# Causal attention with scores as 64-row pairs, output rows straight from turned weights, z on GpSimd, and the next part's loads issued in its last sixteen batches

## What is computed

```python
def _mha(q, k, v):                                   # part c: q = layernorm(x), k = v = ctx, 16 heads of 32 channels
    scores = einsum('bhqd,bhkd->bhqk', qh, kh) / sqrt(hd)
    causal = ki <= qi
    scores = where(causal, scores, -10000.0)
    attn = softmax(scores, axis=-1)
    out = einsum('bhqk,bhkd->bhqd', attn, vh)
x = x + _mha(_layernorm(x), ctx_2048, ctx_2048)
x = x + _L1_ffn_ref(_layernorm(x), workspace, ...)   # part d: starts from all of part c's x
```

## Time and profile before

| | us |
|---|---|
| median of 3 runs | 3930.52 |
| the profiled execution | 3928.73 |
| its span, first to last instruction | 3926.6 |
| TensorE busy in the span | 3598.9 (92%) |
| VectorE busy | 2855.4 (73%) |
| ScalarE busy | 2566.4 (65%) |
| GpSimd busy | 1624.4 (41%) |

### The profile page before, as it was taken

How to read it: one execution, slowest core, us unless ns; L and a number is a source line. 1 busy time by engine, 2 the same in 40 slices (tenths; PEclk the granted TensorE clock), 3 DMA queues, 4 the chain that set the end, 5 groups by cost and what they waited for, 6 DMA issues and landing times. The chain is left out here.

```text
span 3926.6 us, 86340 instructions
## 1 busy us (share of the span) xinstructions
PE 3598.9 (92%) x24389; PEld 1800.9 (46%) x24451; DVE 2855.4 (73%) x4503; ACT 2566.4 (65%) x6417; POOL 1624.4 (41%) x2090
## 2 busy tenths in 40 slices
PE   5999999999999999699999889999995899999997
PEld 1222222222222222477777644444443665566664
DVE  5888888888888889577777667777774446464655
ACT  2777777777777777577776667777774454545454
POOL 6444444444444441566666322222222234242524
PEclk9999999999999999899999999999997999999999
DMA  7777777777777774333333223333334022030402
GB/s 117 122 123 122 122 124 124 122 121 124 121 122 124 123 144 112 109 114 109 110 110 105 70 90 95 97 90 93 97 91 147 11 66 66 26 106 3 130 1 76
DMA packets 344192, 390.16 MB, mean 99 GB/s; under 512 B 58640, under 2 KB 223120, under 8 KB 343952
## 3 DMA queue, kind: packets, MB, share of 16 engines
q1 hardware_dynamic: 317328, 352.82, 41.0%
q10 hardware_dynamic: 26624, 34.63, 3.4%
HBM read 200.65 MB, written 84.93 MB: 73 GB/s over the span
## 5 line engine op out<-in xcount | busy, mean ns | idle before, releaser
L372 DVE TENSOR_REDUCE a_neg_max<-a_max_ps 128x2 f32<-128x1024 f32 x1024 | 1200.1, 1219 | 189.2 <-PE a_max_ps L461 165.6
L493 ACT ACTIVATE a_P<-a_ring_ps 128x512 f32<-128x512 f32 x2048 | 1084.4, 602 | 382.4 <-PE a_ring_ps L443 378.1
L461 PE MATMUL a_max_ps<-a_K,a_Q 96*128 96x512 bf16 x2048 | 620.8, 384 | 44.9 <-DMA a_K<-a_k_split 39.5
L443 PE MATMUL a_ring_ps<-a_Q,a_K 98*128 98x512 bf16 x2048 | 617.6, 382 | 5.0 <-DMA a_Q<-a_max_rows 2.9
L478 PE MATMUL a_pv_ps<-a_P,a_V 128*32 128x512 f32 x4096 | 544.9, 604 | 1.8 <-ACT a_out_sb L498 1.8
L443 PEld LDWEIGHTS a_ring_ps<-a_Q,a_K 98*128 98x128 bf16 x2048 | 157.8, 96 | 657.8 <-ACT a_P L493 584.4
L1181 ACT ACTIVATE c_P<-c_s_ps,c_bias 128x128 f32<-128x128 f32 x1024 | 362.2, 367 | 138.3 <-DVE c_bias L1053 128.1
L1110 PE MATMUL c_s_ps<-c_KD,c_qT 128*128 128x512 f32 x512 | 276.7, 622 | 33.4 <-ACT c_qT L1172 28.8
L1049 DVE TENSOR_REDUCE c_neg_max<-c_s_ps 128x4 f32<-128x512 f32 x256 | 175.5, 685 | 163.5 <-PE c_s_ps L1111 163.5
L461 PEld LDWEIGHTS a_max_ps<-a_K,a_Q 96*128 96x128 bf16 x2048 | 182.3, 98 | 224.9 <-DVE a_neg_max L372 47.5
L319 POOL TENSOR_SCALAR a_var_eps<-a_mean_var 128x1 f32<-128x1 f32 x64 | 12.3, 192 | 644.5 <-DVE a_mean_var L388 644.2
(11 more groups left out here) (251 smaller groups left out, 7084.0 us busy)
## 6 DMA issues: line engine op xcount, KB each, us to landing
a_Q<-a_q_split SPq DMA_DIRECT2D x384, 128.0 KB, 4.6
a_K<-a_k_split SPq DMA_DIRECT2D x384, 128.0 KB, 7.4
heads_out<-a_out_sb ACTq DMA_DIRECT2D x128, 256.0 KB, 3.6
a_x_in<-in_x_dram SPq DMA_DIRECT2D x64, 256.0 KB, 3.6
a_c_in<-in_ctx_dram SPq DMA_DIRECT2D x64, 256.0 KB, 4.1
a_cT_in<-in_ctxT_dram SPq DMA_DIRECT2D x64, 256.0 KB, 4.0
b_x_in<-in_x_dram SPq DMA_DIRECT2D x64, 256.0 KB, 2.8
b_o_in<-heads_out SPq DMA_DIRECT2D x64, 256.0 KB
```

What stands on the lines that cost most here:

```text
L372: dve.tensor_reduce(neg_max[:, p, 2 * u:2 * u + 2], max_ps[u % 2][:, :, :], AX.X, ALU.max, negate=True).then_inc(max_taken, 1)
L443: pe.matmul(ring(s, use_of(k))[:, :], K[i][:, h, n:n + 128], Q[i][:, h, :], start=True, stop=True).then_inc(scores_filled, 1)
L461: last = pe.matmul(max_ps[u % 2][:, j, :], Q[i][0:KROW, h, m:m + 128], K[i][0:KROW, h, :], start=True, stop=True)
L493: act.activation(P[p][k // NT][:, k % NT, :], ring(s, use_of(k))[:, :], ACT.Exp, scale=SCALE).then_inc(exp_done, 1)
```

## The change

1. **Scores.** `KD` keeps two heads a row group (half the size). A chunk's scores are two fp32 matmuls of 64 rows and 256 columns, rows 0 to 63 and 64 to 127, into two banks, and the mask is added by two bf16 matmuls of 256 columns. The four banks now hold two chunks, so S(c) waits for the exps of chunk c - 2.
2. **Output.** `products` has PT as the stationary operand (128 columns) and 32 columns of V moving, and writes output rows directly. The turn of oT and its ScalarE copy are gone; the last chunk's products are issued in the next step, behind S(0).
3. **z on GpSimd**, as the last instruction of its step, in stage 0 instead of stage 1.
4. **Order.** TensorE turns z at c = 2 instead of at the end, and multiplies with `after` at c = 0 instead of c = 1; ScalarE copies qT before the exps of c = 2; VectorE weighs the `after` product at c = 1 and takes moments at c = 3.
5. **The seam.** Part d's tensors and the semaphores that this needs move to a `WorkspaceState` that lives over both parts. SP issues the five weights in steps 48 to 52, the small loads in steps 53 to 56, X in steps 57 to 60. GpSimd does the memsets in step 56 and rstd and x_r in step 64. VectorE makes the constants in steps 57 to 59, the moments of X[0] in steps 60 to 63 and normalises it in steps 64 to 67. For this SP's last 16 steps and GpSimd's and VectorE's last 8 before the drain are written out too.

```diff
-def causal_attention(nc, x, ctx, ctxT, ident, after, causal_cols, x_out):
+def causal_attention(nc, x, ctx, ctxT, ident, after, causal_cols, x_out, w):
...
-        KD = [sb(f"KD{i}", [128, CK, G, 128], F32) for i in range(2)]
+        KD = [sb(f"KD{i}", [128, CK, 2, 128], F32) for i in range(2)]
...
-        s_ps = ps("s_ps", [128, CK, G, 128], F32)
+        s_ps = ps("s_ps", [128, 2, 2, 512], F32)
...
                     for h in range(G):
-                        sp.dma_start(KD[i][h * D:(h + 1) * D, :, h, :],
+                        sp.dma_start(KD[i][h * D:(h + 1) * D, :, h % 2, :],
...
-            pipeline(sp, B, 5, step)
+                if 48 <= t.k < 53:
+                    dst, src = w.big[t.k - 48]
+                    sp.dma_start(dst, src).then_inc(w.big_in, 16)
+                if 53 <= t.k < 57:
+                    for dst, src in w.small[(t.k - 53) * 6:(t.k - 52) * 6]:
+                        sp.dma_start(dst, src).then_inc(w.small_in, 16)
+                if 57 <= t.k < 61:
+                    i, h = (t.k - 57) // 2, (t.k - 57) % 2
+                    for b in range(h * 4, h * 4 + 4):
+                        sp.wait_ge(x3_stored[b % 2], (i * 4 + b // 2 + 1) * 16)
+                        sp.dma_start(w.X[i][:, b, :], w.x[i * 8 + b]).then_inc(w.x_loaded[i][h], 16)
+            pipeline(sp, B, 5, step, ahead=16)
...
                     held.wait_ge(rstd_done, b + 1)
-            pipeline(pool, B, 5, step)
+                    at_least(held, qT_filled, b - 1)
+                    pool.tensor_scalar(z[:, i, :], x_in[:, t.slot(0, 8), :], mean_var[:, i, 0:1], rstd[:, i:i + 1], ALU.subtract, ALU.mult).then_inc(z_done, 1)
+                if t.k == 56:
+                    for n, (dst, value) in enumerate(w.presets):
+                        pool.memset(dst, value).then_inc(w.preset, 1)
+                        pool.wait_ge(w.preset, n + 1)
+                if t.k == 64:
...
+            pipeline(pool, B, 5, step, ahead=8)
...
-                    if t.exists(3) and c == 2:
+                    if t.exists(3) and c == 1:
...
-                    if t.exists(1) and c == 0:
-
-                        b, i, j = t.batch(1), t.slot(1, 2), t.slot(1, 8)
-                        dve.wait_ge(rstd_done, b + 1)
-                        at_least(dve, qT_filled, b - 1)
-                        dve.tensor_scalar(z[:, i, :], x_in[:, j, :], mean_var[:, i, 0:1], rstd[:, i:i + 1], ALU.subtract, ALU.mult).then_inc(z_done, 1)
-                    if t.exists(0) and c == 1:
+                    if t.exists(0) and c == 3:
...
+                if 60 <= t.k < 64:
+                    j = t.k - 60
+                    dve.wait_ge(w.x_loaded[0][j // 2], 64)
+                    for b in range(2 * j, 2 * j + 2):
+                        dve.bn_stats(w.stats[:, b, :], w.X[0][:, b, :]).then_inc(w.stats_done, 1)
...
+                if 64 <= t.k < 68:
+                    dve.wait_ge(w.rstd_done, 1)
+                    for b in range(2 * t.k - 128, 2 * t.k - 126):
+                        dve.tensor_scalar(w.X[0][:, b, :], w.X[0][:, b, :], w.moments[:, b, 0:1], w.rstd[:, b:b + 1],
+                                          ALU.subtract, ALU.mult).then_inc(w.z_done, 1)
...
-                        at_least(pe, exp_done, (b - 1) * H + (c + 1) * G)
-                        pe.matmul(s_ps[:, c], qT[i][:, c, :], KD[i][:, c], start=True, stop=False)
-                        pe.matmul(s_ps[:, c], identb[:, :], farb[:, :].unsqueeze(1).to_broadcast([128, G, 128]),
-                                  start=False, stop=True).then_inc(s_filled, 1)
+                        at_least(pe, exp_done, b * H + (c - 1) * G)
+                        for r in range(2):
+                            rows = slice(r * 64, r * 64 + 64)
+                            pe.matmul(s_ps[:, c % 2, r, 0:256], qT[i][rows, c, :], KD[i][rows, c], start=True, stop=False)
+                        for r in range(2):
+                            last = pe.matmul(s_ps[:, c % 2, r, 0:256], identb[:, :], farb[:, :].unsqueeze(1).to_broadcast([128, 2, 128]),
+                                             start=False, stop=True)
+                        last.then_inc(s_filled, 1)
                     if t.exists(4) and c == 0:
-
-                        b, i = t.batch(4), t.slot(4, 2)
-                        pe.wait_ge(oT_done, b + 1)
-                        for k in range(CK):
-                            last = pe.transpose(bank_b[:, k, :], oT[:, i, k, :], identf[:, :])
-                        last.then_inc(o_filled, 1)
+                        products(t, 4, CK - 1)
...
-                    last = pe.matmul(bank_b[g * D:(g + 1) * D, c, :], V[t.slot(3, 4)][:, h * D:(h + 1) * D], PT[i][:, h, :],
+                    last = pe.matmul(bank_b[:, h * D:(h + 1) * D], PT[i][:, h, :], V[t.slot(back, 4)][:, h * D:(h + 1) * D],
...
-                if t.exists(3):
-                    b, i = t.batch(3), t.slot(3, 2)
-                    act.wait_ge(oT_filled, b + 1)
-                    at_least(act, o_filled, b - 1)
-                    act.activation(oT[:, i], bank_b[:, :, :], ACT.Copy).then_inc(oT_done, 1)
```

More of the change, by code:

```diff
@@ new lines, in step @@
+                if 60 <= t.k < 64:
[3 more added lines that the diff above has]
+                        dve.bn_stats(w.stats[:, b, :], w.X[0][:, b, :]).then_inc(w.stats_done, 1)
+                    for b in range(2 * j, 2 * j + 2):
+                        dve.wait_ge(w.stats_done, b + 1)
+                        dve.bn_aggr(w.moments[:, b, :], w.stats[:, b, :]).then_inc(w.moments_done, 1)
@@ L1095, in _ @@
+                if 64 <= t.k < 68:
[3 more added lines that the diff above has]
+                                          ALU.subtract, ALU.mult).then_inc(w.z_done, 1)
+            pipeline(dve, B, 5, step, ahead=8)
         @block.tensor
@@ L1127, in step, with products @@
                         if c > 0:
-                            products(t, c - 1)
-                        if c == 1:
-                            pe.wait_ge(qT_done, min(b + 2, B) if isinstance(b, int) else b + 2)
-                            pe.matmul(bank_a[:, :, :], after_sb[:, :], V[t.slot(3, 4)][:, :], start=True, stop=True).then_inc(mv_filled, 1)
-                if t.exists(1):
-                    b, i = t.batch(1), t.slot(1, 2)
-                    pe.wait_ge(z_done, b + 1)
-                    at_least(pe, masked_v_done, b - 1)
-                    for c in range(CK):
-                        last = pe.transpose(bank_a[:, c, :], z[:, i, c * 128:(c + 1) * 128], identf[:, :])
-                    last.then_inc(qT_filled, 1)
-                if t.exists(3):
-                    products(t, CK - 1)
-            def products(t, c):
-                b, i = t.batch(3), t.slot(3, 2)
+                            products(t, 3, c - 1)
+                    if t.exists(3) and c == 0:
+                        b = t.batch(3)
+                        pe.wait_ge(v_loaded[t.slot(3, 4)], t.lap(3, 4) * 16 + 16)
+                        pe.wait_ge(qT_done, min(b + 2, B) if isinstance(b, int) else b + 2)
+                        pe.matmul(bank_a[:, :, :], after_sb[:, :], V[t.slot(3, 4)][:, :], start=True, stop=True).then_inc(mv_filled, 1)
+                    if t.exists(1) and c == 2:
+                        b, i = t.batch(1), t.slot(1, 2)
+                        pe.wait_ge(z_done, b + 1)
+                        at_least(pe, masked_v_done, b - 1)
+                        for k in range(CK):
+                            last = pe.transpose(bank_a[:, k, :], z[:, i, k * 128:(k + 1) * 128], identf[:, :])
+                        last.then_inc(qT_filled, 1)
+            def products(t, back, c):
+                b, i = t.batch(back), t.slot(back, 2)
                 if c == 0:
-                    pe.wait_ge(v_loaded[t.slot(3, 4)], t.lap(3, 4) * 16 + 16)
                     at_least(pe, o_sum_done, b)
@@ L1422, in step @@
             def step(f, u, after):
-                if f.exists() and not f.second():
+                if f.exists() and not f.second() and f.k != 0:
                     e = f.eight()
@@ L1581, in normalise @@
                                           ALU.subtract, ALU.mult).then_inc(z_done, 1)
-                first = f.exists() and not f.second()
+                first = f.exists() and not f.second() and f.k != 0
                 if first:
@@ L1977, in decoder @@
         ternary_ffn(nc, x, ffn, x2)
[L1978 to L1980 removed]
+    with ExitStack() as st:
+        w = WorkspaceState(nc, st, x3, ident, workspace, compete_wT, compete_b, write_wT, write_b, wq, wkT, wvT, in_proj_cols,
+                           out_wT, out_b, pre_cols, norm_post)
+        causal_attention(nc, x2, ctx, ctxT, ident, after, causal_cols, x3, w)
+        workspace_ffn(nc, x3, w, out)
 def kernel(**inputs):
```

200 lines of the change are left out of this document (111 added, 89 removed).

## The result

The new kernel takes 3835.34 us (median of 4 runs, 3834.83 to 3841.88), the old one beside it 3928.59 (4 runs): ratio 0.9767, with a 95% interval of 0.975 to 0.9784. It is faster, as forecast, and inside the range, but the gain is 93 us where the forecast had 50, and the time lies 5 us under what the prediction called its likeliest case alone (3840 to 3905). The profiled spans stand 94.1 us apart (3926.6 and 3832.5).

What follows compares the result with a forecast made beforehand. TensorE's program order, with two holes per batch, was taken to bound the causal part. 3928.7 - 32 (step) - 28.4 (seam) - 1.8 (memsets) + 11 (last steps) + 0.6 (semaphores) = 3878 us, range 3805 to 3968.

Steps and rivals of the forecast that it cites:

- Seam: Start of part d: TensorE begins about 0.4 us after the barrier, at 3004.3 instead of 3032.75; -28.4 us.
- The last steps: Last sixteen causal batches: VectorE's borrowed constants and moments delay P^T's first copy 1.6 us in seven steps; +11 us.
- The step: One causal batch on TensorE: 10.8 us instead of 11.31, over 63 batches; -32 us.
- P = 0.92: A chunk's products: eight passes at 0.115 us each, 0.92 us instead of 0.36.
- T = 0.53: A chunk's four transposes of P on TensorE: 0.53 us, before and after.
- S = 0.90: A chunk's scores with mask: 0.90 us, with 0.25 for entering and leaving 64-row mode; bounds 0.75 and 1.08.
- KD's smaller memsets: Ahead of the first loads: two memsets of 3.67 us halve as KD is half as large; -1.8 us.
- One more clearing of semaphores: At the kernel's end: one additional clearing; +0.6 us.
- Rival 1: Causal batches: GpSimd's z shuts VectorE out, TensorE stands 1.45 us a batch, step 12.25, 3960 us; chance 0.22.
- Rival 2: Products: full weight loads not hidden, at least 192 ns a pass, step 13.3, 4020 us; chance 0.05.
- Rival 3: Products: weight loads cheap, 0.08 us a pass, step 9.7, 3808 us; chance 0.12.
- Rival 4: Scores: 64-row pairs don't overlap, 1.08 us or more a chunk, step 11.5, 3922 us; chance 0.05.

Runs made afterwards that it cites:

- Run 3: New kernel with z moved back from GpSimd to VectorE, in the next step's first chunk: 3828.85 us (0.9747).
- run 4: New kernel with each chunk's scores again one product of 128 rows and 512 columns, two banks in turn: 3869.31 us (0.9853).
- run 2: Old kernel's causal batches, with the next part's loads, memsets, constants and moments in their last sixteen steps as in the change: 3912.18 us (0.9955).
- run 11: New kernel with the next part's VectorE, GpSimd and SP work spread over the last sixteen steps: 3828.26 us (0.9742).
- run 10: New kernel with qT turned at the end of the step again (TensorE and ScalarE at c = 3): 3891.92 us (0.99).
- run 5: New kernel with products as before (V as weight), the result turned back, ScalarE's copy of oT ahead of exp(0): 3788.49 us (0.9646).
- run 6: New kernel plus one unread VectorE bn_stats per batch ahead of total, so total starts under GpSimd's z: 3874.23 us (0.9859).
- run 7: run 6 with GpSimd's z replaced by two tensor_tensor additions, results not the reference's: 3914.95 us (0.9966).
- run 8: run 5 with ScalarE's copy of qT behind the exps of chunk 2 instead of ahead: 3786.65 us (0.9636).

## Why the prediction was right, and where its size was wrong

- **The bound.** PE's program order set the step before and sets it after. Shown by runs 3 and 4: a full us more on DVE changes nothing, 0.64 more on PE changes the step by 0.64.
- **Seam.** -28.4 forecast, -28.6 found. Run 2 shows it for itself, less its late steps.
- **The last steps.** +11 forecast, +8 found. That DVE's lump delays P^T's first copy was right, and run 11 shows it. The forecast's 1.6 us a step, seven times, was not: it lets POOL's z hold `bias` and `total` on top. In the trace z held `bias` behind the first two lumps (0.68 at 2838.80 and 2849.73) and neither of the two behind the last four (0.23 each). Six steps lost 0.4 to 1.4 us, and one lost 3.2, with a wait of 1.17 us and the slow clock behind it, which the forecast did not have. That the sum came near is partly luck.
- **The step, -32 forecast, some -70 found.** This is the sum whose terms were mis-sized. The largest error is **P = 0.92**. The rate was nearly right: 0.115 a pass forecast, 0.112 found. But the forecast charged it eight times, and it is paid seven times, because the first load of a group runs under the transposes in front: 0.031 + 7 x 0.112 = 0.81. That is -0.11 x 4 = -0.44. The second is **T = 0.53**. That figure of the earlier trace rows was read with products in column groups behind it, and holds the way into them. The same timeline of before has a T with full scores behind it, and there, up to the scores at 2402.82, it takes 0.43:

```profile
2402.39 0.60 PE L1125 MATMUL c_pT_ps<-c_identf,c_P 128*128 128x128 f32 x4
```

In the new kernel T is 0.44, so -0.09 x 4 = -0.36, and -0.06 on the turn of z. Against these stands **S = 0.90**, which is 0.97 with its way in: +0.07 x 4 = +0.28. So T and S nearly cancel: the price of the way in stood in T where it belonged to S. 10.79 - 0.44 - 0.36 - 0.06 + 0.28 = 10.21, and 10.19 is measured. The low bound of the step, 9.95, held it.
- **Parts of the 70.** Undone one at a time, the pairs are worth 34 us (run 4), the place of z's turn 57 (run 10) and the products -47 (run 5): 44 together. The other 26, with the vanished wait for oT's copy among them, no run has for itself, and such parts need not add up.
- **Holes.** That qT's copy is hidden by the new place was argued with 0.3 us to spare; the trace has no wait, and run 10 brings it back at 1.0 us a step. The move stands for more than the "0.52" that the rows of before showed.
- **KD's smaller memsets.** They take 1.96 instead of 3.67, but the stretch from the part's first memset to S(0) is 11.37 us, 0.29 longer than before. The first z on POOL lasts 2.07 where DVE took 0.55, and while the pipeline fills nothing covers it. Run 3, with z back on DVE, has 9.41 there, 1.7 less than before. So the -1.8 was right and z on POOL took it away; the fill was left out of the sum.
- **One more clearing of semaphores, +0.6.** No run shows this term. Behind the seam the new trace is 0.35 us shorter, and the time around the span is 2.3 instead of 2.1.
- **Rival 1** (z shuts DVE out) was not met in the steady stretch, because `total` starts 0.44 ahead of z (2603.55 and 2603.99). Had it been met, its price was wrong: by run 6 it is 0.55 at most, within P^T's slack of 0.64, and not 1.45. The earlier trace rows showed the lock with an addition, and run 7 shows it with additions again; I had carried it to an instruction of another form. The Trainium skill (SBUF — State Buffer, "SBUF: two separate sides") speaks of an exclusive lock between DVE and GpSimd. Run 7 agrees with it (2609.75 beside 2609.73), run 6 only for z's first 0.78 us.
- **Rival 2** (full loads not hidden, 0.192 a pass) is refuted by 0.112. (Its 4020 was also added wrongly: 3878 + 32 + 126 is 4036.) The rule of the Trainium skill (TensorE: Matmul & The Clock Gate, Part 3, "The mechanism") that a load overlaps matmuls only in another row group does not hold here: these loads and passes are all in one. The same section also has loads pulled ahead into a background weight buffer, which would fit.
- **Rival 3**'s 3808 is nearer to 3835 than the forecast's 3878, but its cause is not what happened: a pass takes 0.112, not 0.08. **Rival 4** (pairs don't overlap) is refuted by run 4 and by the starts 0.007 us apart.

## What to carry to other kernels

Read an operation's length between the neighbours that it will have: the same transposes took 0.53 ahead of column groups and 0.44 ahead of full ones. Where a run of equal passes is paced by its weight loads, count the intervals and not the passes, as the first load can lie under what runs in front: eight passes took 0.81 and not 8 x 0.115. Undo each part of a bundle for itself: this one won by the order of its instructions, the scores and the seam, while the part that seemed its centre, output rows without turning, cost 47 us against turning them with the copy in a better place. Work borrowed from the next stage belongs in the idle places of a step, one piece each, and not at its end in a lump.

## What the runs showed of the hardware that was not expected

- A GpSimd addition of 128x512 holds a DVE `scalar_tensor_tensor` of 128x16 until it ends (run 7); a GpSimd `tensor_scalar` with two scalars per row (mean and rstd), 2.08 us long, holds it only until 0.78 us behind its own start (run 6).
- The DVE's own z of 128x512 takes 0.54 us in the first three batches of the kernel before, with GpSimd idle, and 0.96 to 1.00 in most others, where it starts some 0.35 us into GpSimd's multiplication.
- A 128-column fp32 weight load shows as 192 ns but allows a new pass every 0.112 us, if 32 columns move.
- Ahead of 64-row groups the last pass in front takes 0.09 to 0.10 us longer (the product with `after`, the turns and the products all show it). A pass of 256 columns in a pair takes 0.31 where a full one takes 0.215. Full fp32 scores behind 32-column passes also start 0.09 slower.
- One PE wait of 1.17 us was followed by some 7 us at a granted clock of 0.50, and one of 1.06 (run 6, at 2885.3) by 13.7 us. Waits of 0.26 in most steps (run 6) and of 0.8 to 0.9 in every step (run 10) were not, and neither were single ones of 1.64 (run 8) and 2.07 (run 2). So the length of a wait alone doesn't decide it.
